# A post-norm decoder layer on one core: residual and moments three steps behind their tile in place of two, exponentials ahead of the row splits

## The reference

```python
x = _layernorm(x + _L0_attn_ref(x, ...))
x = _layernorm(x + _L0_xattn_ref(ctx_2048, x, mask, mask, ...))
x = _layernorm(x + _L0_ffn_ref(x, w1, b1, w2, b2))
# inside _L0_attn_ref: t = 8 positions, b = 512 rows, 16 heads of 32
ac = jnp.einsum('tbhd,sbhd->bhts', q + r_w_bias, k)
bd = _rel_shift(jnp.einsum('tbhd,rhd->bhtr', q + r_r_bias, p))[..., :t]
attn = jax.nn.softmax((ac + bd) * scale, axis=-1)
ctx = jnp.einsum('bhts,sbhd->tbhd', attn, v).reshape(t, b, e)
return ctx @ out_proj_weight.T + out_proj_bias
```

## Time and profile before

| | |
|---|---|
| median of 3 runs | 1947.03 us (1946.83 to 1951.03) |
| the profiled execution | 1940.6 us |
| its span, first to last instruction | 1938.8 us |
| TensorE matmul, busy share of the span | 94% |
| VectorE, busy share | 68% |
| ScalarE, busy share | 41% |
| GpSimd, busy share | 29% |
| mean granted TensorE clock | 0.983 of full |

### The profile page before, as it was taken

The page is one execution under the profiler, slowest core; times in us unless marked ns, Lnnn a source line. Parts: engine busy times, 40 slices in busy tenths (PEclk is TensorE's granted clock), DMA queues, the critical chain, the costliest instruction groups (busy, mean ns, idle before and its releaser), DMA issues. The chain is left out here.

```text
span 1938.8 us, 33279 instructions
## 1 busy us (share of the span) xinstructions
PE 1831.4 (94%) x12476; PEld 1002.7 (52%) x12476; DVE 1321.6 (68%) x1670; ACT 787.7 (41%) x1209; POOL 559.8 (29%) x574
## 2 busy tenths in 40 slices
PE   5999999999999999868899999999999999999998
PEld 5556545645554665435455455454554554544543
DVE  3488999899989989767465554655655546546521
ACT  3432222222222222247465364463653645636522
POOL 1334874486449327700101102003011020030010
PEclk8999999999999999989999999999999999999999
DMA  6554447435643456565411505307116053061010
GB/s 224 119 120 104 93 109 171 116 83 127 162 109 87 126 142 152 148 143 183 85 53 37 123 23 93 89 1 128 53 39 121 22 99 82 1 130 30 12 33 22
DMA packets 321298, 183.97 MB, mean 95 GB/s; under 512 B 225258, under 2 KB 278506, under 8 KB 321155
## 3 DMA queue, kind: packets, MB, share of 16 engines
q1 hardware_dynamic: 316784, 181.52, 38.8%
q10 hardware_dynamic: 4370, 0.34, 0.2%
HBM read 94.75 MB, written 33.55 MB: 66 GB/s over the span
## 5 line engine op out<-in xcount | busy, mean ns | idle before, releaser
L1416 DVE TENSOR_TENSOR p_lo<-k,p_hi 128x1024 f16<-128x1024 f32 x128 | 156.9, 1225 | 193.6 <-ACT p_hi L1289 193.6
L1061 POOL TENSOR_TENSOR q<-q,x_hi 128x512 f16<-128x512 f32 x28 | 37.6, 1372 | 639.3 <-ACT x_hi L1342 639.3
L1461 DVE CUSTOM_DVE_ANT_0 junk<-b_sx,mneg 128x512 f16<-128x512 f32 x256 | 176.0, 688 | 32.1 <-issue 23.3
L1089 PE MATMUL b_ff<-x2T_hi,w1T_hi 128*128 128x512 f16 x512 | 194.7, 380 | 1.9 <-DVE x2T_lo L1416 1.9
L1089 PE MATMUL b_ff<-x2T_lo,w1T_hi 128*128 128x512 f16 x512 | 194.6, 380 | 0.0
L1089 PE MATMUL b_ff<-x2T_hi,w1T_lo 128*128 128x512 f16 x512 | 194.6, 380 | 0.0
L1321 ACT ACTIVATE k<-b_st,mbias 128x512 f32<-128x512 f32 x256 | 161.6, 685 | 14.5 <-PE b_st L1135 13.9
L745 DVE TENSOR_TENSOR prod<-q,k 128x4096 f32<-128x4096 f32 x32 | 147.6, 4612 | 13.0 <-ACT q L677 12.1
L1289 ACT ACTIVATE p_hi<-k 128x1024 f16<-128x1024 f32 x128 | 135.3, 1057 | 44.8 <-PE b_av L1150 42.4
L1313 ACT ACTIVATE hq<-b_ff,b 128x512 fp8e4<-128x512 f32 x128 | 88.0, 687 | 155.6 <-PE b_ff L1089 148.6
L595 PE MATMUL pj_b<-winT_hi,xT_hi 128*128 128x512 f16 x384 | 146.5, 382 | 3.8 <-DMA xT_lo<-rows_lo 3.8
(11 more groups left out here) (260 smaller groups left out, 4363.1 us busy)
## 6 DMA issues: line engine op xcount, KB each, us to landing
cn<-in_ctx_dram SPq DMA_DIRECT2D x64, 256.0 KB, 3.1
k<-kT_scratch SPq DMA_DIRECT2D x24, 512.0 KB, 7.6
xn<-in_x_dram SPq DMA_DIRECT2D x32, 256.0 KB, 2.9
x<-in_x_dram SPq DMA_DIRECT2D x32, 256.0 KB, 3.1
x_scratch<-x SPq DMA_DIRECT2D x32, 256.0 KB, 2.2
q<-x_scratch SPq DMA_DIRECT2D x8, 1024.0 KB, 5.7
q<-x_scratch SPq DMA_DIRECT2D x32, 256.0 KB, 2.9
out_dram<-q SPq DMA_DIRECT2D x32, 256.0 KB, 4.4
```

Source lines behind the costliest of these rows:

```text
L1089: mm = pe.matmul(out, a, c, start=(start and n == 0), stop=end)
L1416: dve.tensor_tensor(dst, bank, hi, ALU.subtract).then_inc(out, 1)
L1461: dve.tensor_tensor_reduce(junk[:, :], sx_b[tt % 2][:, :], mneg[:, :], 1.0, NEG, ALU.add, ALU.max, mx[:, h % 2, tt:tt + 1]).then_inc(s["sx ...
```

## The change

Five loops use a later step for the same tile: the residual and moments on VectorE at `g - 3` in place of `g - 2`, the factors on GpSimd and `normalize` on ScalarE at `g - 4` in place of `g - 3`, the store on SyncE at `g - 5` in place of `g - 4`, and the load of the residual tile at `g - 2` in place of `g - 1`. There is one more step at the end for it. TensorE's order stays as it was. Apart from that, the exponentials stand ahead of the row splits at place 8 of ScalarE's order.

```diff
 class FirstHalf:
-    STEPS = 16 * NB + 4
+    STEPS = 16 * NB + 5
...
             for g in range(plan.STEPS):            # SyncE
-                for n in plan.tiles(g - 4):
+                for n in plan.tiles(g - 5):
                     store_x1(n)
...
-                for n in plan.tiles(g - 1):
+                for n in plan.tiles(g - 2):
                     load_residual(n)
...
             for g in range(plan.STEPS):            # GpSimd
-                for n in plan.tiles(g - 3):
+                for n in plan.tiles(g - 4):
                     norm_factors(n)
...
             for g in range(plan.STEPS):            # ScalarE
+                if g % 16 == 8 and g < 16 * NB:
+                    exponentials(g // 16)
                 for use in plan.uses(g):
                     row_hi(*use)
-                if g % 16 == 8 and g < 16 * NB:
-                    exponentials(g // 16)
...
-                for n in plan.tiles(g - 3):
+                for n in plan.tiles(g - 4):
                     normalize(n)
...
                     score_sums(b, t)               # VectorE, and twice more below
-                    for n in plan.tiles(g - 2):
+                    for n in plan.tiles(g - 3):
                         residual_and_moments(n)
```

## The result

The changed kernel takes 1942.63 us (median of 11 runs, 1938.11 to 1945.68), the kernel before 1948.41 us beside it (11 runs, 1945.21 to 1954.53): ratio 0.9965, 95% interval 0.9952 to 0.9978. The same two kernels a second time gave 0.9968 (0.9956 to 0.998). So the change gains 0.35%, some 6.8 us by the ratio (the two medians alone are 5.8 us apart), where I had forecast 0.41%. The time lies near the forecast, but the profile does not show the way there that I had reckoned.

What follows compares the result with a forecast made beforehand. TensorE (598.6 of 618.0 us busy) and VectorE (576.7) were both nearly full. Waits removed, less step 20's 5.6 us and later slips, netted block by block to -8.0: 1932.6 us profiled, 1939.0 median, range 1934 to 1951.

Steps and rivals of the forecast that it cites:

- step 17: Step 17 of the first half: TensorE's stall of 2.98 us was taken to show no clock loss.
- the store in step 20: Step 20: the store delays the context transposes, adding 3.9 us of TensorE stall and 1.7 of clock loss, 5.6 in all.
- the exponentials and the projection: VectorE's softmax waits of 5.36, 7.70, 3.60 us fall to 2.2, 0.5, 0.5; its projection waits of 2.95, 2.39, 1.49 go.
- `om_used`, which I had put at zero: Context half: the output projection's new wait for the residual one step later, taken as zero, bounds zero and 1.55 us.
- the rows for step 37 are wanted a whole quarter later: Steps 36 and 37: argument against a full TensorE stall there, leaving it late by only some 0.4 us.
- the slip of step 36: Step 36: context transposes go 3.6 us later, costing TensorE 0.4 us and leaving VectorE 2.8 us late.
- rival 2: TensorE keeps the gain: step 36 costs a full stall, 4.9 us more, the end at -3, 1944 us; chance 0.26.
- The signs that I had named for being wrong: TensorE stalls over 2 us in steps 36, 37 or 52 to 54, none in step 20, or a new `om_used` wait.
- each residual less in a context half makes its sums 1.55 us earlier: Context halves: five residuals in place of six, each some 1.55 us of VectorE, bring a block's context sums 1.55 earlier.
- the rule for this contention: Score halves: VectorE and GpSimd block each other's port; worst order some 0.5 us in each of three blocks, sum -6.5.
- the tail: End of the first half: the last residual tile loads behind a store it waits for, 0 to 1 us, taken 0.2.

## Why the prediction was right in the time and wrong on the way

I give TensorE's lead P and VectorE's lead D as the start of an instruction in the first profile after, less that of the same one before. The 0.85 us from ahead of the first softmax is in every lead.

| place | forecast | measured |
|---|---|---|
| end of context half 1 | P -3.1 | P -3.7, then -2.3 behind step 17 |
| behind step 20 | P +2.5 | P +2.9 |
| softmax 2 | D -0.5 | D -0.2 |
| end of context half 2 | P +0.3, D -1.5 | P +0.2, D -0.2 |
| step 37 | P +0.7, D +2.8 | P +0.5, D +2.6 |
| behind step 40 | not in the sum | P +5.0 |
| softmax 3 | D -4.4 | D -1.4 |
| end of context half 3 | P -4.3, D -6.1 | P -0.5, D -0.9 |
| softmax 4 | D -5.1 | D -1.5 |
| end of context half 4 | P -6.8, D -8.2 | P -1.7, D -1.9 |
| start of the second half | -8.0 | -0.7 |

**Right: the store in step 20.** The forecast was a stall of 5.8 us by 1.76 from the copy to the transposes and 3.93 from there to the quarter. ScalarE and SyncE in the changed kernel:

```profile
308.22 0.60 ACT L677 ACTIVATE v<-pj_b 128x512 f32<-128x512 f32 x1 [2.18 <-PE pj_b L596]
```

```profile
309.54 0.34 SPq L495 DMA_DIRECT2D x_scratch<-x  x1
309.98 1.22 SPq L466 DMA_TRANSPOSE cT_hi<-rows_hi  x1
```

308.22 to 309.98 is 1.76, and 309.98 to 313.87 is 3.89; the stall is 5.75. The clock of 0.83 over the 10 us behind it, between the levels of 1.2 and 2.4 GHz, makes 1.7 us, the value that I took from the earlier trace rows. The sum of 5.6 came out at 5.2.

**Right: the exponentials and the projection.** The exponentials start at 354.43, 537.22 and 715.29 us, and the waits of the earlier trace rows became 2.19, 0.68 and 0.48 us (forecast 2.2, 0.5, 0.5). No wait for `om_b` is left in a context half, TensorE has none for `om_used`, which I had put at zero, its waits for `c1T` in the first three context halves are 0.6 us in place of 10.3, and the stall of 3.88 is 3.29.

**Wrong: "the rows for step 37 are wanted a whole quarter later".** With this I let the slip of step 36 end at 0.4 us, and so far it held: the transposes go 3.7 us later (forecast 3.6), TensorE waits for 0.21 at 501.91, and VectorE is 2.6 us late. What failed is that I ended the account there. The slip went on through stage stores, loads and splits, and reached TensorE at 534.82, in step 40: 2.62 us, and a clock of 0.88 over 14 us, 1.7 more. P goes from +0.5 to +5.0. This is rival 2 in price (4.9 us, with an end at -3), though not in place; its term was the one missing from my sum. Removing the stores' wait shows it: the stall is gone with all stores moved and 1.64 with that of step 36 alone. The signs that I had named for being wrong did not catch it: no stall of over 2 us stands in steps 36, 37 or 52 to 54.

**Wrong in size: step 17.** I took its stall of 2.98 as costing no clock. In the changed kernel the same stall, 2.96, is followed by matmuls of 0.37 in place of 0.27, and P falls from -3.7 to -2.3: 1.4 us. The loss does not need the change: the second profile of before lost 1.1 us behind the same stall, with a clock of 0.83 over the 10 us from 279. Of the eight profiles that have this stall of 2.95 to 2.99 us, five show a clock of 0.83 or 0.84 over the 10 us behind it (one of the three without the residual part, four of the five with it) and three show 1.00. The larger error was to take this stall, and the 1.89 in step 20, as given. Taking away the wait behind them is worth 0.8% in the kernel before, 7.4 to 8.2 us in the profiles.

**Wrong: each residual less in a context half makes its sums 1.55 us earlier.** In the third step of the fourth context half one is gone and D moves by only 0.6. VectorE's context sum and two merged splits of GpSimd in the changed kernel:

```profile
746.38 3.25 DVE L790 TENSOR_TENSOR prod<-prod 128x2048 f32<-128x2048 f32 x1
```

```profile
746.33 4.31 POOL L549 TENSOR_TENSOR rows_lo<-cn,rows_hi 128x512 f16<-128x512 f32 x2
```

In the kernel before this sum takes 2.26 and starts behind the residual, when GpSimd's first two splits of the step are done. The groups of the two sum lines over the first half show it as a whole, before and then after (busy us, mean ns):

```profile
L790 DVE TENSOR_TENSOR prod<-prod 128x2048 f32<-128x2048 f32 x32 | 75.8, 2369 | 0.1
L792 DVE TENSOR_TENSOR prod<-prod 128x1024 f32<-128x1024 f32 x32 | 41.7, 1303 | 1.1
```

```profile
L790 DVE TENSOR_TENSOR prod<-prod 128x2048 f32<-128x2048 f32 x32 | 79.0, 2468 | 0.1
L792 DVE TENSOR_TENSOR prod<-prod 128x1024 f32<-128x1024 f32 x32 | 47.6, 1486 | 1.1
```

9.1 us more of VectorE for the same work, and 8.5 in the second profile. It comes with the residual part: the two lines together take 117.5 to 119.1 us in the five profiles without it and 124.0 to 126.6 in the nine with it. (The score products, L745, give some back: 147.6 before, 143.5 after.) I had weighed the rule for this contention, but only for the norm factors in the score halves. In the same half the wait of 1.49 went as forecast, but a wait for `stage_hi` just ahead of it grew from 1.01 to 1.92 (784.34), and D moved by 0.5 there.

**Wrong in size: the tail.** For the residual tile of the last step, loaded just behind a store that it must wait for, I took 0.2 us out of 0 to 1. The last residual before, then SyncE and the last residual after:

```profile
826.50 0.69 DVE L802 SCALAR_TENSOR_TENSOR x<-om_b,x 128x512 f32<-128x512 f32 x1 [6.80 <-PE om_b L606]
```

```profile
819.58 0.43 SPq L495 DMA_DIRECT2D x_scratch<-x  x1
822.90 0.34 SPq L491 DMA_DIRECT2D x<-in_x_dram  x1
```

```profile
825.83 0.69 DVE L802 SCALAR_TENSOR_TENSOR x<-om_b,x 128x512 f32<-128x512 f32 x1 [1.89 <-DMA x<-in_x_dram]
```

From TensorE's last stall to the start of the second half it is 9.3 us before and 10.4 after: 1.0 us, the upper bound. It is 9.1 to 9.3 us in the five profiles without the residual part and 10.1 to 10.5 in the nine with it. In six of the nine the last projection also ran slower (5.1 us from its first to its last matmul, in place of 3.9 to 4.2); in the other three it took 2.6 to 4.0, and the distance was 10.1 to 10.5 us all the same.

**The time.** The 7.3 us between -8.0 and -0.7 come together in this way. P is 4.3 us later than forecast behind step 40, and 3.6 of that are left in D at the fourth softmax. The last context half adds 2.7 to D, of which 1.0 is the sum above, 1.0 the wait for `stage_hi`, and the rest lies in smaller pieces that I did not follow. The tail adds 0.8, and 0.2 is that P, not D, ends the half. The profiled executions took 1943.3 and 1944.6 us, against 1940.6 and 1944.0 before: by them the change gains nothing. (In the first pair 3.3 us of this is the second half, 1107.6 us before and 1110.9 after with the same program.) I had carried the sum over to the median by adding what lies between the profiled execution of before and its runs, 6.4 us. That gap is no constant. The median lies 6 to 8 us above the profiled execution for the kernel before and 4.4 above for the one with the exponentials alone, but 0.6 and 2.3 us below it for the changed one, whose runs have a clock of 0.975 to 0.979, and within 3.5 us either way for all others. So the measured gain of 6.8 us is time that the timed executions of before lose and its two profiled ones do not, and every ratio above holds it, and my forecast of 1939.0 came near 1942.6 by two errors that offset each other. That the time came out near was luck. The pairs of clocks above, in the third context half and in step 17, show two places of this kind; where in the timed runs it happens is open, since they leave no trace.

## What to carry to other kernels

Where one engine issues DMAs in order, a store whose data comes from the far end of another engine's step must not stand ahead of loads or transposes that the busiest engine wants next. Here moving the store was worth as much by itself as the better part of the change (7.4 us against 7.2 in the profiles) and 17 us in the changed kernel, and it decided whether a later residual helps or hurts. Follow a slip in such a queue until it is used up, not to its first reader. And an engine's idle time is worth removing only as long as that engine leads the bound: the same wait for the exponentials was worth 0.64% in the kernel before and nearly nothing with the store behind the transposes and the residual one step later. And when a forecast is made against one profiled execution, the distance to the timed runs is a number of that kernel, not a constant to be carried over.

## What the runs showed of the hardware

GpSimd's split of 128x512 took 1.16 us where it started ahead of VectorE's product and 4.14 to 4.53 where it started behind it, and VectorE's sum took 3.25 in place of 2.26 us where GpSimd had started just before. By the Trainium skill, SBUF — State Buffer, section "SBUF: two separate sides", the port pair that the two share goes to whichever starts first, for its whole instruction, when VectorE reads two SBUF inputs. The rows agree: the split that started at 510.62 ended 1.0 us behind the end of the product (514.76 against 513.74), nearly the 1.16 that it takes by itself. What I had not expected is the size in a kernel that is full on both sides: starting times that move by 1 us change a split by 3 us.

The same stall of 2.98 us in the same program had a clock of 1.00 behind it in one execution and 0.74 in the other; on one chip one program ran from 1941 to 1958 us, at mean clocks from 0.983 to 0.976. Two profiles of one kernel were too few to tell a difference of 0.3% from this.
